# A decoder layer's first microseconds: the head mask filled first, products of ones ahead of the weight folds, one token load alone

## The reference, cut to what matters

```python
# 1: chunked linear attention, 16 heads of 16 features
q, k, v = proj(wq), proj(wk), proj(wv)                    # x @ w.T, split into heads
q = (q @ fq1_w.T + fq1_b) * (q @ fq2_w.T + fq2_b)
k = (k @ fk1_w.T + fk1_b) * (k @ fk2_w.T + fk2_b)
...                                                       # causal scores, RMS norm per head, times norm_w
x = layernorm(x + o @ wo.T)
# 2: long convolution of x * ctx with a filter by head (by FFT), skip term, product with ctx
x = layernorm(x + conv(x, skip, ctx, ctx, 8))
# 3: feed-forward part with 4-bit weights, 256 -> 2048 -> 256
x = layernorm(x + (gelu(x @ Wg.T) * (x @ Wu.T)) @ Wd.T)
```

## Time and profile before

| | us |
|---|---|
| median of 3 runs | 573.89 |
| the runs | 573.31, 573.89, 574.43 |
| the profiled execution, its own time | 574.71 |
| its span, first to last instruction | 572.4 |

### The profile page before, as it was taken

How to read it: one execution, slowest core, us unless ns; L and a number is a source line. 1 busy time by engine, 2 the same in 40 slices (tenths; PEclk the granted TensorE clock), 3 DMA queues, 4 the chain that set the end, 5 groups by cost and what they waited for, 6 DMA issues and landing times.

```text
span 572.4 us, 9307 instructions
## 1 busy us (share of the span) xinstructions
PE 539.1 (94%) x3385; PEld 439.7 (77%) x3385; DVE 375.3 (66%) x782; ACT 148.0 (26%) x259; POOL 123.3 (22%) x195
## 2 busy tenths in 40 slices
PE   5999979989989999999999999999999997699993
PEld 5766757766878888776888888866888885588883
DVE  3998888975876577875455668875454778533334
ACT  3422200252333112232232111332333110222230
POOL 2100078210002445120003444120003451200001
PEclk9999899999999999999999999999999999599998
DMA  5532342130110110023001110040001110100001
GB/s 173 156 80 79 89 118 66 38 111 2 48 45 29 46 50 26 0 78 108 1 1 38 56 40 16 0 147 0 0 0 46 55 46 2 37 1 0 1 0 37
DMA packets 25249, 26.69 MB, mean 47 GB/s; under 512 B 2816, under 2 KB 22784, under 8 KB 25216
## 3 DMA queue, kind: packets, MB, share of 16 engines
q1 hardware_dynamic: 14208, 15.73, 9.3%
q10 hardware_dynamic: 10576, 8.95, 5.1%
q0 software_dynamic: 432, 1.57, 0.8%
HBM read 24.15 MB, written 2.10 MB: 46 GB/s over the span
## 4 chain that ended last, share of the span: by engine, by line
PE 82%; DVE 9%; DMA 3%; issue 2%; POOL 1%; ACT 1%; ACTq 0%; POOLq 0%; DVEq 0%; SPq 0%
PE bank L911 17%; PE bank L913 15%; PE bank L912 15%; PE front_bank L1030 5%; PE front_bank L1033 4%; PE front_bank L1031 4%; PE front_bank L972 4%; PE front_bank L959 3%; PE bank L906 3%; PE front_bank L911 2%; PE front_bank L912 2%; PE front_bank L913 2%; PE front_bank L1004 2%; DVE st L719 1%; DMA wo_sb<-in_woT 1%
## 5 line engine op out<-in xcount | busy, mean ns | idle before, releaser
L911 PE MATMUL bank<-x2T_lo,ffn_hi 128*128 128x512 f32 x256 | 111.6, 436 | 4.1 <-DVE x2T_lo L838 4.1
L854 DVE TENSOR_TENSOR inter<-bank,inter 128x512 f32<-128x512 f32 x64 | 44.2, 690 | 95.6 <-PE bank L913 95.3
L913 PE MATMUL bank<-x2T_hi,ffn_hi 128*128 128x512 f32 x256 | 102.2, 399 | 0.0
L912 PE MATMUL bank<-x2T_hi,ffn_lo 128*128 128x512 f32 x256 | 101.9, 398 | 0.0
L436 POOL TENSOR_TENSOR qbd<-qT_sb,ctxT_sb 128x256 f32<-128x256 f32 x128 | 77.8, 631 | 76.8 <-PE front_bank L1033 63.3
L386 POOL TENSOR_TENSOR ve<-ve,minus_half 128x2 f32<-128x2 f32 x24 | 17.4, 743 | 301.0 <-DVE ve L726 229.8
L911 PE MATMUL bank<-ffn_lo,inter_hi 128*128 128x256 f32 x256 | 77.2, 302 | 0.8 <-DVE inter_lo L848 0.8
L588 ACT ACTIVATE inter_hi<-inter 128x512 fp32r<-128x512 f32 x64 | 40.4, 632 | 143.0 <-DVE inter L854 143.0
L582 ACT ACTIVATE inter<-bank 128x512 f32<-128x512 f32 x64 | 38.2, 598 | 134.5 <-PE bank L913 134.5
L913 PE MATMUL bank<-ffn_hi,inter_hi 128*128 128x256 f32 x256 | 72.0, 281 | 0.0
L912 PE MATMUL bank<-ffn_hi,inter_lo 128*128 128x256 f32 x256 | 71.9, 281 | 0.0
(11 more groups left out here) (115 smaller groups left out, 795.3 us busy)
## 6 DMA issues: line engine op xcount, KB each, us to landing
toep_sb<-in_toep ACTq DMA_DIRECT2D x64, 128.0 KB, 2.1
xT_sb<-in_xT SPq DMA_DIRECT2D x4, 512.0 KB, 6.3
ctxT_sb<-in_ctxT SPq DMA_DIRECT2D x4, 512.0 KB, 4.4
x_sb<-in_x SPq DMA_DIRECT2D x4, 512.0 KB, 5.3
ctx_sb<-in_ctx SPq DMA_DIRECT2D x4, 512.0 KB, 6.3
out<-ctxT_sb POOLq DMA_DIRECT2D x3, 512.0 KB, 3.4
raw_w<-in_gate_p SPq DMA_DIRECT2D x8, 128.0 KB
raw_s<-in_gate_s SPq DMA_DIRECT2D x8, 128.0 KB
```

The costliest lines, as they stand in the source:

```text
L854: nc.vector.tensor_tensor(inter[:, n % 2, :], up_ps[:, :], inter[:, n % 2, :], ALU.mult).then_inc(inter_ready, 1)
L911: nc.tensor.matmul(ps, w_hi, x_lo, start=start, stop=False, skip_group_check=True)
L912: nc.tensor.matmul(ps, w_lo, x_hi, start=False, stop=False, skip_group_check=True)
L913: return nc.tensor.matmul(ps, w_hi, x_hi, start=False, stop=stop, skip_group_check=True)
```

## The change

POOL fills a new tile `ones`, then `head_one`, `skip_mat`, `ident`, `causal`, `minus_half`, waits for these five, cuts the masks in the order of before, and fills `v_sb` last. PE first makes eight 128 x 128 products of `ones` with itself into `down_ps[1]`, which nobody reads, and then the folds, each waiting only for its own raw weight (`ld_wq`, `ld_wk`) and its own factor. DVE waits for one mask instead of four ahead of `f_bd`; the wait for the small loads, the scaled bias, the scaled `skip_mat` and the scaled `wo_sb` move behind the splits. The loads of `wv_sb` and `wo_sb` move from ACT's queue to SP's: `wv_sb` is issued once `xT_sb` has landed, ahead of `fetch(0)`, and `wo_sb` behind `fetch(1)`. PE's waits for `wv_sb`/`wo_sb` ahead of the turn go; the one for DVE's eight constants moves to `vproj`.

```diff
@@ sync
-            sp.dma_start(raw_wq, wq.rearrange("(k p) n -> p k n", p=P)).then_inc(ld_fold, 16)
-            sp.dma_start(raw_wk, wk.rearrange("(k p) n -> p k n", p=P)).then_inc(ld_fold, 16)
+            sp.dma_start(raw_wq, wq.rearrange("(k p) n -> p k n", p=P)).then_inc(ld_wq, 16)
+            sp.dma_start(raw_wk, wk.rearrange("(k p) n -> p k n", p=P)).then_inc(ld_wk, 16)
             load_xT(0, 0)
...
+            sp.wait_ge(ld_xT, 16)
+            sp.dma_start(wv_sb[:], wvT.rearrange("(k p) n -> p k n", p=P)).then_inc(ld_wv, 16)
             fetch(0)
             fetch(1)
+            sp.dma_start(wo_sb[:], woT.rearrange("(k p) n -> p k n", p=P)).then_inc(ld_wo, 16)
             load(0)
@@ gpsimd
+            nc.gpsimd.memset(ones[:], 1.0).then_inc(ones_ready, 1)
+            nc.gpsimd.memset(head_one[:], 1.0).then_inc(filled, 1)
+            nc.gpsimd.memset(skip_mat[:], 1.0).then_inc(filled, 1)
             nc.gpsimd.memset(ident[:], 0.0).then_inc(filled, 1)
             nc.gpsimd.memset(causal[:], 1.0).then_inc(filled, 1)
-            nc.gpsimd.memset(head_one[:], 1.0).then_inc(filled, 1)
-            nc.gpsimd.memset(skip_mat[:], 1.0).then_inc(filled, 1)
             nc.gpsimd.memset(minus_half[:], -0.5).then_inc(filled, 1)
-            nc.gpsimd.memset(v_sb[:], 0.0).then_inc(filled, 1)
-            pool.wait_ge(filled, 6)
+            pool.wait_ge(filled, 5)
...
+            nc.gpsimd.memset(v_sb[:], 0.0).then_inc(filled, 1)
@@ scalar
-            act.dma_start(wv_sb[:], wvT.rearrange("(k p) n -> p k n", p=P)).then_inc(ld_wo, 16)
-            act.dma_start(wo_sb[:], woT.rearrange("(k p) n -> p k n", p=P)).then_inc(ld_wo, 16)
...
-            act.wait_ge(ld_wo, 32)
+            act.wait_ge(ld_wv, 16)
@@ vector
             dve.wait_ge(ld_factors, 16)
-            dve.wait_ge(const_ready, 4)
+            dve.wait_ge(const_ready, 1)
...
-            dve.wait_ge(ld_small, 32)
             nc.vector.tensor_copy(head_sel[:], head_one[:, :, 0]).then_inc(dve_const, 1)
...
-            nc.vector.tensor_scalar(skip_mat[:], skip_mat[:], skip_sb[:, 0:1], None, ALU.mult).then_inc(dve_const, 1)
-            nc.vector.tensor_scalar(b_small[:, 5:6], b_small[:, 1:2], DK ** -0.5, None, ALU.mult).then_inc(bd_ready, 1)
-            dve.wait_ge(ld_wo, 32)
-
-            nc.vector.tensor_scalar(wo_sb[:], wo_sb[:], b_small[:, 4:5], None, ALU.mult).then_inc(dve_const, 1)
             for i in range(4):
                 if i == 2:
                     split_x(0)
+                    dve.wait_ge(ld_small, 32)
+                    nc.vector.tensor_scalar(b_small[:, 5:6], b_small[:, 1:2], DK ** -0.5, None, ALU.mult)\
+                        .then_inc(bd_ready, 1)
...
                 .then_inc(wvlo_ready, 1)
+            dve.wait_ge(const_ready, 4)
+            nc.vector.tensor_scalar(skip_mat[:], skip_mat[:], skip_sb[:, 0:1], None, ALU.mult).then_inc(dve_const, 1)
+            dve.wait_ge(ld_wo, 16)
+
+            nc.vector.tensor_scalar(wo_sb[:], wo_sb[:], b_small[:, 4:5], None, ALU.mult).then_inc(dve_const, 1)
             dve.wait_ge(dve_const, 8)
@@ tensor
-            pe.wait_ge(ld_fold, 32)
+            pe.wait_ge(ones_ready, 1)
+            for _ in range(8):
+
+                nc.tensor.matmul(down_ps[1][:, 0:P], ones[:], ones[:], start=True, stop=True, skip_group_check=True)
             for i in range(4):
                 pe.wait_ge(dve_const, i + 1)
+                pe.wait_ge(*((ld_wq, 16) if i < 2 else (ld_wk, 16)))
...
-            pe.wait_ge(ld_wo, 32)
-            pe.wait_ge(dve_const, 8)
@@ tensor, vproj
                     if isinstance(g, int) and g == 0:
                         pe.wait_ge(wvlo_ready, 1)
+                        pe.wait_ge(dve_const, 8)
```

More of the change, by code:

```diff
@@ L85, in decoder_layer @@
         minus_half = sb("minus_half", [P, 1])
+        ones = sb("ones", [P, P])
         with ExitStack() as early:
@@ L147, in sems @@
             return [sem(n) for n in names]
-        ld_fold, ld_wo, ld_factors, ld_small, ld_xT, ld_x, ld_ctxT, ld_ctx, stored = sems(
-            "ld_fold", "ld_wo", "ld_factors", "ld_small", "ld_xT", "ld_x", "ld_ctxT", "ld_ctx", "stored")
+        ld_wq, ld_wk, ld_wv, ld_wo, ld_factors, ld_small, ld_xT, ld_x, ld_ctxT, ld_ctx, stored = sems(
+            "ld_wq", "ld_wk", "ld_wv", "ld_wo", "ld_factors", "ld_small", "ld_xT", "ld_x", "ld_ctxT", "ld_ctx", "stored")
         ld_w = sems("ld_w_even", "ld_w_odd")
@@ L176, in decoder_layer @@
         spread_ready = sems("spread_even_ready", "spread_odd_ready")
-        filled, const_ready, pool_mask, kv_ready, prod_ready = sems(
-            "filled", "const_ready", "pool_mask", "kv_ready", "prod_ready")
+        ones_ready, filled, const_ready, pool_mask, kv_ready, prod_ready = sems(
+            "ones_ready", "filled", "const_ready", "pool_mask", "kv_ready", "prod_ready")
         last_mm, last_stored = sems("last_mm", "last_stored")
```

## The result

| | before | changed |
|---|---|---|
| median, us | 573.89 | 576.51 |
| runs | 13, 573.03 to 576.87 | 13, 575.83 to 578.22 |
| ratio to before, 95% interval | | 1.0045 (1.0031 to 1.0059) |
| span of the profiled execution | 572.4 | 574.5 |

The change makes the kernel 0.45% slower, 2.6 us. The forecast was 1.4 us faster.

A forecast was written before the change was run, and what follows sets the result against it. The prediction took the start to be bound by a chain from `wo_sb`'s landing to piece 2's scales, then PE alone. Piece 2 starting 1.35 us earlier made 573.89 into 572.5 us, range 571.5 to 574.2.

The forecast's parts named there:

- Folds, ones, splits: Start of kernel on PE, ACT, DVE: folds end at 9.0 instead of 11.6, first projection starts 3.0 us earlier.
- SP's queue: Load issues on SP: `ctxT_sb` 1.6 us earlier, `wo_sb` landing at 12.6, so piece 0 starts 1.7 earlier, at 13.1.
- DMA: Loads up to piece 2's scales: stream at 284 GB/s, 0.9 us earlier; scales land at 19.0, piece 2 starts 1.35 earlier.
- bound by their issue: Piece 2's scale load: 3.47 us behind `ctx` loads against 3.33 with nothing before, so its issue time sets its landing.
- The wait on SP: SP waits for `xT_sb` (7.0) before issuing `wv_sb`, fetches and `wo_sb`; DMA queue empty until 8.15.
- The third one: Rival: `wo_sb`, behind SP's wait and four loads, lands at 16.7; piece 0 starts at 17.2; 576.3 us; chance 0.1.
- The second rival: TensorE's clock falls while PE pauses ahead of projections 3 and 7; net gain 0 to 0.75 us; chance 0.1.
- The sum: Whole kernel: piece 2's 1.35 us earlier start is saved in full, giving a median of 572.5 us.
- The paragraph on moving loads between engines: Skill's rule: all engines' DMAs share 16 DMA engines, so moving two loads from ACT to SP moves no byte faster.
- The first rival: Stream up to piece 2's scales: bytes decide, only 0.6 us or less of idle DMA time saved; chance 0.24.

The follow-up runs named there:

- e3: Changed kernel with the 4-bit weights' scales laid out in HBM once per partition (128 rows instead of 8 spread by the load); 0.9963 of the kernel before.
- e1: Changed kernel with `wo_sb` issued right behind `wv_sb`, ahead of `fetch(0)` and `fetch(1)`; 1.0030 of the kernel before.
- e11: e2 with SP's wait for `xT_sb` put back ahead of `fetch(0)`; 1.0022 of the kernel before.
- e2: Changed kernel with `wv_sb` and `wo_sb` issued by ACT at the start and no wait for `xT_sb` on SP; 0.9965 of the kernel before.
- e6: Changed kernel without SP's wait for `xT_sb`, all loads staying on SP's queue in their new order; 0.9947 of the kernel before.
- e13: Changed kernel as it is, timed again beside e14; median 577.48 us, 1.0054 of the kernel before.
- e14: Changed kernel with 24 unread products behind projection 2 to fill PE's pause, second timing; median 577.14 us, 1.0040 of the kernel before.
- e4: Changed kernel with DVE's wait for `wo_sb` and its scaling moved to piece 5 of the unpacking; 1.0065 of the kernel before.

## Why the prediction was wrong

- **Folds, ones, splits: right.** Ones from 1.20 to 4.99 (forecast 1.2 to 4.6), folds to 8.8 (9.0), `xT_sb` at 6.8 (7.0), first projection at 9.14 (9.6). DVE stood ready for `wo_sb` at 11.65 (12.4).
- **SP's queue: the issues right, the landing wrong.** `wo_sb` was issued at 9.67 (9.6), `ctxT_sb` at 10.18 (10.1). The step that failed is "`wo_sb` lands at 9.6 + 3.0 = 12.6, by the 3.0 of `wq`": it took 6.55 and landed at 16.2. `wq` had nothing ahead of it; `wo_sb` had two fetches. With their scales laid out by partition it took 4.0 (e3), ahead of them 3.1 (e1).
- **DMA: the rate wrong.** I took 284 GB/s for the 1.05 MB of `wv_sb`, fetches and `wo_sb`, the rate of a stream of `ctx` loads. 139 GB/s came in 9 to 12.5. The rows that warned of it were there and were read for something else: 128 KB of scales in 3.33 us with only their codes ahead, against 256 KB in 3.0. I read the 3.33 as a latency ("bound by their issue") when it was in part the price of a slow transfer. Before the change the fetches were issued at the very start, beside ACT's queue, and had landed long before anybody waited.
- **The wait on SP.** I counted one empty us and the issue times of four loads as its price. The idle time was right (29 GB/s in 7 to 8). Missing was that the slow transfers are pushed from a time when nothing waits to a time when `wo_sb`, the `ctx` loads and `fetch(2)` stand behind them. e11 prices the wait at 0.57% over e2, 3.3 us, the clock's fall included; on one queue, e6 prices it at 5.6.
- **The rivals.** The third one, `wo_sb` as the bound, gave 16.7, 17.2 and 576.3; measured are 16.2, 16.8 and 576.5. It had a chance of 0.1. It named the right load, but its 7.14 was that of another queue among other loads, so that it comes within 0.6 of the measured 6.55 is luck; and e1 shows that its place isn't the only one: with `wo_sb` in time, piece 2's scales are still 0.9 late. The second rival came true on top: the clock fell, over a pause of 5.7 us instead of the 1.5 that I had, and cost about 1.1 (e13 against e14).
- **The sum.** First scores 2.9 us late in the profiled execution: 2.0 from piece 0, 0.9 from PE at the lower level (DVE waits 0.91 us for PE ahead of projection 3's epilogue). The median moved 2.6, the spans 2.1: in the traces 0.7 of the delay is given back between 480 and 500 us, around a stretch at the lower level (0.50) that is 13.7 us long in the profiled execution before and 10.3 in the changed one.
- **The paragraph on moving loads between engines** was sound as far as it went: e2 and e6, which differ in the queue, can't be told apart. The first rival's 0.6 us of idle time, built on it, was not what decided.

## What to carry to other kernels

A wait that lets one load run alone doesn't only delay what stands behind it: here it moved the slowest transfers of the queue to where others were waited for. Before reordering loads, divide the bytes by the time of each load kind with nothing beside it; a load that takes longer for half of the bytes should be issued first or given another layout, and here the layout was worth as much as the whole reorder was meant to be. And when a wait is taken off an in-order engine, look at what its next wait is (here piece 2's scales), since e1 and e4 removed the named wait and gained nothing that the intervals show.

## What the runs showed of the hardware that was not expected

- Loads that spread 8 rows over 128 partitions are slower than as many bytes from 128 rows (3.33 against 2.3 us for the same load), and hold up what is queued behind them: in 9.0 to 12.5, in the same order of loads, 139 against 246 GB/s were moved in all. They also delay loads of another queue: PE waits 1.64 us for `toep_sb`, and not at all with the other layout.
- With 24 matmuls added in the first 20 us, PE stalled some 340 us later, at the end of the loop, for 1.76 and 1.65 us, in both profiled executions of that kernel and in no other here. The cause is open.
